# First attention pass: the expansion as one product of 24 columns a place, its three parts added on VectorE

## What is computed

```python
h = (x @ W).reshape(n, HEADS, HID)                  # HEADS = 4, HID = 64
a_src = jnp.einsum('nhf,hf->nh', h, att_src)
a_dst = jnp.einsum('nhf,hf->nh', h, att_dst)
e = jax.nn.leaky_relu(a_src[src] + a_dst[dst], NEG_SLOPE)
m = jax.ops.segment_max(e, dst, num_segments=n)
ex = jnp.exp(e - m[dst])
denom = jax.ops.segment_sum(ex, dst, num_segments=n)
alpha = ex / denom[dst]
msg = h[src] * alpha[:, :, None]
agg = jax.ops.segment_sum(msg, dst, num_segments=n)
```

## Time and profile before

| | |
|---|---|
| median of 3 runs | 8563.55 us (8562.0 to 8572.29) |
| the profiled execution | 8565.55 us, its span 8563.6 us |
| mean granted clock of TensorE | 0.757 of full speed |
| busy, share of the span | TensorE 62%, its weight loads 55%, VectorE 66%, ScalarE 36%, GpSimd 71% |
| the first attention pass | first reduction at 2476.8, last scores at 3701.5 us |
| in that pass | 58 batches, each with 48 matmuls of the expansion |

### The profile page before, as it was taken

How to read it: one execution, slowest core, us unless ns; L and a number is a source line. 1 busy time by engine, 2 the same in 40 slices (tenths; PEclk the granted TensorE clock), 3 DMA queues, 4 the chain that set the end, 5 groups by cost and what they waited for, 6 DMA issues and landing times. The chain is left out here.

```text
span 8563.6 us, 137030 instructions
## 1 busy us (share of the span) xinstructions
PE 5287.4 (62%) x37370; PEld 4671.1 (55%) x37370; DVE 5613.1 (66%) x13450; ACT 3042.1 (36%) x7001; POOL 6100.7 (71%) x5620
## 2 busy tenths in 40 slices
PE   0991014444368888763444415655579898989896
PEld 0340013333346666563333315655579898989896
DVE  9661025555578888763444455555579898989898
ACT  2000002000048888732222222222256666666564
POOL 4777767777647777727777727777768787878785
PEclk6995555555578888886666657677689999999998
DMA  1771015565645555623333324444567676767674
GB/s 43 271 308 54 2 46 130 131 145 131 118 111 139 138 136 138 123 66 79 82 79 82 79 48 130 129 129 130 123 172 221 189 222 190 222 189 222 189 222 138
DMA packets 962997, 1176.44 MB, mean 137 GB/s; under 512 B 286474, under 2 KB 845278, under 8 KB 949198
## 3 DMA queue, kind: packets, MB, share of 16 engines
q1 hardware_dynamic: 806638, 864.50, 33.2%
q0 software_dynamic: 155616, 303.19, 16.6%
HBM read 897.16 MB, written 269.96 MB: 136 GB/s over the span
## 5 line engine op out<-in xcount | busy, mean ns | idle before, releaser
L2572 PE MATMUL ps<-u,wide_r 128*128 x9280 | 1141.9, 277 | 128.7 <-issue 89.0
L2572 PEld LDWEIGHTS ps<-u,wide_r 128*128 128x128 f32 x9280 | 1093.6, 194 | 130.7 <-issue 130.7
L2147 POOL DMA_INDIRECT z_r<-x_tab,src_row x880 | 852.6, 969 | 417.5 <-issue 267.8
L2584 PE MATMUL ps<-msg_r,hots_r 128*128 128x128 f32 x9280 | 1135.5, 275 | 21.5 <-POOL msg_r L2405 21.5
L2405 POOL TENSOR_TENSOR msg_r<-zo_r,share_r 128x1024 f32<-128x1024 f32 x580 | 1123.1, 1936 | 11.8 <-DVE share_r L2457 9.0
L1356 POOL DMA_INDIRECT ring_e<-t_tab,src_p x928 | 878.9, 947 | 322.7 <-issue 269.7
L2584 PEld LDWEIGHTS ps<-msg_r,hots_r 128*128 128x128 f32 x9280 | 1082.6, 192 | 26.7 <-POOL msg_r L2405 25.3
L296 POOL DMA_INDIRECT rec_tab<-pay,row_i x831 | 806.3, 970 | 375.0 <-issue 274.3
L584 POOL DMA_INDIRECT ring<-y_tab,y_row x880 | 839.4, 954 | 306.0 <-issue 266.2
L2413 POOL TENSOR_TENSOR prod_r<-prod_r 128x512 f32<-128x512 f32 x580 | 735.0, 1267 | 415.9 <-DVE prod_r L2435 414.6
L1767 POOL DMA_INDIRECT ring_e<-t_tab,src_row x880 | 830.7, 944 | 271.9 <-issue 271.9
(11 more groups left out here) (320 smaller groups left out, 9520.7 us busy)
## 6 DMA issues: line engine op xcount, KB each, us to landing
zo_r<-zo_tab SPq DMA_DIRECT2D x2320, 192.0 KB, 2.8
y_tab<-wide SPq DMA_DIRECT2D x100, 1024.0 KB, 3.9
zo_tab<-z_r SPq DMA_DIRECT2D x110, 512.0 KB
hot_bytes_e<-hb_tab SPq DMA_DIRECT2D x464, 64.0 KB
dl_b<-dl_tab SPq DMA_DIRECT2D x220, 128.0 KB, 3.8
zo_tab<-hot_bytes SPq DMA_DIRECT2D x220, 128.0 KB, 2.3
hb_tab<-hot_bytes SPq DMA_DIRECT2D x220, 128.0 KB, 2.3
hot_bytes_e<-hb_tab SPq DMA_DIRECT2D x55, 512.0 KB
```

Source lines behind the costliest of these rows:

```text
L2147: nc.gpsimd.indirect_dma_start(out=z[:, g % ZR, c, :], out_offset=None, in_=x3_tab, in_offset=bass.IndirectOffsetOnAxis(ap=src_row[:, g * ...
L2572: last = nc.tensor.matmul(ps[:, 2 * (g % 2) + c // 4, c % 4 * D:(c % 4 + 1) * D], wide[:, g % WR, c, :], u[:, bass.ds(tiles[g % NO % 4 * O ...
L2584: last = nc.tensor.matmul(ps[:, 4 + g % 2, c // 2 * D:(c // 2 + 1) * D], hots[:, g % WR, c, :], msg[:, g % WR, c, :], start=c % 2 == 0, st ...
```

## The change

The three matmuls of a chunk become one with 24 columns, which leaves the three parts side by side in PSUM: 16 chunks x 24 = 384 columns of the bank. A reduction on VectorE at the head of `scores` adds the three parts (its innermost axis k has a stride of 8 words) into a new SBUF tile `sent`, 16 x 8. The three score instructions wait for it by a new semaphore and read it instead of PSUM. The orders of all engines are otherwise as they were.

```diff
+                sent = sb(f"sent_{name}", [P, BC, 2 * HEADS], fp32, ph)
...
+                s_sent = sem(f"expanded_parts_added_{name}", ph)
...
-                def sent_of(b):
-                    return ps[:, 6 + b % 2, 256:256 + BC * 2 * HEADS].rearrange("p (c w) -> p c w", w=2 * HEADS)
+                SW = 3 * 2 * HEADS
+
+                def expanded(b):
+                    return ps[:, 6 + b % 2, 0:BC * SW]
...
-                            v.tensor_tensor(sc, sent_of(b)[:, :, 0:HEADS], ring[:, b % ZR, :, hf:W], ALU.add)\
+                            v.tensor_reduce(sent[:].rearrange("p c w -> p (c w)"),
+                                            expanded(b).rearrange("p (c k w) -> p c w k", c=BC, k=3),
+                                            AX.X, ALU.add).then_inc(s_sent, 1)
+                            dve.wait_ge(s_sent, b + 1)
+                            v.tensor_tensor(sc, sent[:, :, 0:HEADS], ring[:, b % ZR, :, hf:W], ALU.add)\
                              .then_inc(s_sc, 1)
...
-                            v.tensor_tensor(sc, sc, sent_of(b)[:, :, HEADS:2 * HEADS], ALU.subtract).then_inc(s_sc, 1)
+                            v.tensor_tensor(sc, sc, sent[:, :, HEADS:2 * HEADS], ALU.subtract).then_inc(s_sc, 1)
...
                             for c in range(BC):
-                                for k in range(3):
-                                    last = nc.tensor.matmul(
-                                        sent_of(b)[:, c, :], wide[:, b % WR, c, :],
-                                        sent_b[:, b % 2, bass.ds(tiles[b][c // 2], 1), k, 1:4 * HEADS:2]
-                                        .rearrange("p t w -> p (t w)"), start=k == 0, stop=k == 2)
+                                last = nc.tensor.matmul(
+                                    expanded(b)[:, c * SW:(c + 1) * SW], wide[:, b % WR, c, :],
+                                    sent_b[:, b % 2, bass.ds(tiles[b][c // 2], 1)]
+                                    .rearrange("p t k w -> p (t k w)")[:, 1:2 * SW:2], start=True, stop=True)
                             last.then_inc(s_exp, 1)
```

## The result

The change makes the kernel slower: 8624.9 us in the median of four runs (8620.4 to 8625.9), against 8567.2 us of four runs of the kernel before, a ratio of 1.0068 (95% interval 1.0056 to 1.0080), 58 us. The profiled execution took 8625.9 us with a span of 8624.0. The prediction was 8608: the direction and the range were right, but 44 us were forecast and 58 came.

The account below looks back on a forecast made before the run. The prediction took a loop through several engines in the first attention pass as the bound. 55 batches x (0.60 sum + 0.20 clock) = 44 us on the profiled 8565.55, less 2.0 for the median, gave 8608 us; range 8586 to 8628.

Parts of the forecast that it names:

- The loop, and its end: First attention pass: scores, exponential, messages, first total, add and VectorE's own work form a loop without slack, 20.47 us a batch.
- TensorE's part at nothing: Expansion: 16 matmuls instead of 48 take off 1.95 us per batch, costed at nothing because VectorE is busy until then.
- The sum at 0.60: VectorE ahead of the scores: the added reduction, 562 ns plus some 30, puts 0.60 us per batch wholly on the loop.
- PSUM or SBUF as the scores' source, at nothing: First and third score instructions: reading the sums in SBUF instead of PSUM changes nothing; the skill's figures would win about 7 us.
- The clock's part at +0.20 a batch: TensorE's totals and spreads: the slow clock stretch lies otherwise, between -1.45 and +1.15 us per batch, taken as +0.20.
- slow pair: A TensorE total and the spread behind it at half clock, about 2.75 us; a further one loses a batch 1.15 us.
- Held at 20.47: Rival for the batch length: the clock gives back just what the sum takes, 8564 us; chance 0.06.
- The rival "faster": The slow stretch leaves the first total, which starts at full clock; gathers then bind at 20.0 us, 8538 us; chance 0.05.
- GpSimd's wait: Sign in the gathers: GpSimd's wait for the total, once a batch, grows from 0.78 us to over 1.2.
- The stage's end: Two batches near the end, where VectorE waits 6.44 and 29.74 us for something outside the loop, would swallow their additions.

## Why the prediction was right, and where its size was off

- **The loop, and its end.** Right. Scores, exponential, first total, add and VectorE's row of work set the batch; each time on it moved as it should (ScalarE's wait 2.79 to 3.35).
- **TensorE's part at nothing.** Right in the result, and shown alone: batch 20.48 and 8567.7 us with the short expansion and no sum. The wait for the turn's data grew by 2.8 us, where 2.6 were forecast; the 16 matmuls took 0.64 us, 40 ns each, where 61 were assumed. The reason given was not quite so: an earlier end of the expansion does release the scores, by 0.07 to 0.08 us a batch. This brought no time because the batch is held.
- **The sum at 0.60.** Mis-sized, but little: 0.562 forecast and 0.548 measured for the reduction, and 0.56 us instead of 0.60 for the step, since the sum begins sooner behind the maximum than the scores did, which is the shorter expansion's share. In 55 batches that is 31 us instead of 33.
- **PSUM or SBUF as the scores' source, at nothing.** Right within what the traces can tell: with its sums in SBUF the first score instruction has a median of 276 ns in the profile of the change but 225 in two other profiles of the same instruction, and the third takes 225 (220 with PSUM); with PSUM the first takes 225, and 215 with the short expansion. Why it is longer in the one profile stays open. The Trainium skill ("VectorE: DVE Perf Modes", the section on the TRN2 errata) has the SBUF source cheaper by 62 cycles; no trace here shows it cheaper.
- **The clock's part at +0.20 a batch.** This is the step that failed in size: it is 1.14 - 0.56 = 0.58 us. I had put one further slow pair into one batch of six. The trace has it in one batch of three, at 1.4 us (22.4 against 21.0), and half of one in another (21.5 against 21.0), as two of three slow stretches last 10.2 us instead of 6.8. The reason I gave, less work in the quiet time, was wrong: the sum with 48 matmuls has the same batches and nearly the same clock (0.80 against 0.79), and the short expansion without the sum keeps the 0.83 of the kernel before. A longer loop is enough, whatever makes it longer. That the term came out as a loss at all was luck, since the side was chosen for that reason; 8624.9 lies 3 us inside the upper end of the range, which had allowed for a slow pair in every other batch.
- **The rival "Held at 20.47"** named the true mechanism and drew the wrong result from it. The batch is held by the clock. But it is held only against a loop that gets shorter or stays. The sum lengthens the loop from the end of the flat, and there a step costs about twice its length (0.60 for 0.26, 1.14 for 0.56).
- **The rival "faster"** asked whether the first total starts at full clock. It does so in some batches of the kernel with 80 filling matmuls, and these take 19.44 us. In the change it never does: the first total takes 2.10 us in every batch from 5 to 50.
- **GpSimd's wait** was forecast above 1.2 us and is 1.27 to 2.67 in the rows shown. The stage's end swallowed about 3 us (33.0 us of waits for 36.2).

## What to carry to other kernels

Where a loop's length repeats to a hundredth and one engine's clock drops once in each turn, take neither a cut nor an addition at its own length: here 0.26 us less was worth nothing, and 0.26 more cost 0.60. Measure the slope first, with one dummy instruction more and one fewer in the chain. And a cheaper step on an engine that is not last brings no time by itself. Filling the room that it left with matmuls that nobody reads took the changed kernel from 0.68% slower to 0.25% faster, but only the way back to the held 20.48 us is explained: the rest came from shorter waits near the stage's end, with one size of filling and not with a smaller one, and its cause is open.

## What the runs showed of the hardware

- The batch of 20.48 us (20.478, 20.482, 20.482 and 20.477 in four kernels whose loops differ by 0.78 us in length) is held by TensorE's clock. In the kernel before, the granted clock falls once a batch, in TensorE's quiet time behind the expansion (3030.11), and rises 6.83 us later, while it works on the second total. When the loop gets shorter, the totals meet more of the half clock: the second total takes 1.46, 1.55 and 1.72 us at steps of 0, -0.08 and -0.27. With the loop at +0.56 us the slow stretches change in a turn of three batches, 64.9 us long.
- Matmuls that nobody reads count for the clock too: 110 of them in a batch raised the mean granted clock from 0.79 to 0.92.
- A memset that nothing waits for, 0.11 us by itself, put 0.01 us into a chain of dependent instructions on average. A sum of 548 ns, with the wait for it, put in 0.59 us with the long expansion in place.
- A score instruction of 64 elements with all operands in SBUF takes from 224 to 299 ns, with a median of 276 in one profile and 225 in two others; with an operand in PSUM it takes 214 to 226.
